# Leaving out waits that other waits contain: a layer kernel (linear attention, then a 4-bit feed-forward) on one core

## What is computed

```python
q, k, v = (split_heads(x @ W + b) for W, b in ((Wq, bq), (Wk, bk), (Wv, bv)))
q, k = (exp(z - max(z)) / (sum(exp(z - max(z))) + EPS) for z in (q, k))
context = ((q @ k.T) / (sum(q) + EPS)) @ v
x = layernorm(x + context @ Wo + bo)
h = silu(fp4_linear(x, w_gate)) * fp4_linear(x, w_up)
x = layernorm(x + fp4_linear(h, w_down))      # fp4_linear rounds both operands
```

## Time and profile before

| | |
|---|---|
| median of 3 runs | 809.0 us (808.98 to 809.23) |
| the profiled execution | 809.8 us |
| its span, first to last instruction | 808.0 us |
| busy: PE, DVE, ACT, POOL | 734.5, 728.9, 577.6, 573.4 us |
| attention loop, passes | 17.1 to 17.7 us each |
| feed-forward loop, passes | 30.0 us each |
| granted TensorE clock, mean | 0.979 |

### The profile page before, as it was taken

One profiled execution on the slowest core, in us unless ns is written; L12 is line 12 of the kernel. 1 busy time (PEld: TensorE's weight loads), 2 busy tenths in 40 slices (PEclk: granted clock), 3 DMA queues, 4 the chain that ended last, 5 costly groups with the idle time before them and its releaser, 6 DMA issues.

```text
span 808.0 us, 19912 instructions
## 1 busy us (share of the span) xinstructions
PE 734.5 (91%) x4964; PEld 689.5 (85%) x4964; DVE 728.9 (90%) x1778; ACT 577.6 (71%) x1547; POOL 573.4 (71%) x617
## 2 busy tenths in 40 slices
PE   4999999999999968799999999999999999999994
PEld 4898888888888847699899899899889889889983
DVE  4989999999999988799999999999999999998883
ACT  3577777778777767477667767677777767767666
POOL 3776666666666655678778878878778788788761
PEclk9999999999999969799999999999999999999998
DMA  4122222222222100000000000000000000000002
GB/s 131 60 72 80 60 71 65 65 65 69 74 70 64 43 27 1 1 1 2 7 21 20 15 19 19 13 19 19 16 17 19 19 13 19 19 13 21 21 21 73
DMA packets 39717, 29.20 MB, mean 36 GB/s; under 512 B 3446, under 2 KB 39676, under 8 KB 39676
## 3 DMA queue, kind: packets, MB, share of 16 engines
q1 hardware_dynamic: 37228, 26.50, 10.6%
q10 hardware_dynamic: 2448, 2.23, 0.9%
HBM read 20.32 MB, written 8.39 MB: 36 GB/s over the span
## 4 chain that ended last, share of the span: by engine, by line
PE 53%; DVE 24%; issue 15%; ACT 2%; POOL 2%; DVEq 2%; DMA 0%; POOLq 0%; ACTq 0%; SPq 0%
PE bank L849 36%; PE wide L849 5%; PE bank L911 3%; DVE ln_u L629 3%; PE bank L857 3%; DVE scratch L837 3%; DVE ln_t L627 3%; DVE scratch L824 2%; PE wide L898 2%; DVE scratch L808 2%; PE wide L952 2%; PE bank L909 2%; DVE scratch L779 1%; DVE rounded L830 1%; DVE res L767 1%
## 5 line engine op out<-in xcount | busy, mean ns | idle before, releaser
L849 PE MATMUL bank<-wf_hi,rounded 128*128 128x352 f32 (+1 forms) x1792 | 411.3, 312 | 34.2 <-DVE rounded L830 21.7
L849 PEld LDWEIGHTS bank<-wf_hi,rounded 128*128 128x128 f32 x1792 | 302.9, 191 | 46.6 <-DVE rounded L830 29.1
L849 PE MATMUL bank<-wf_lo,rounded 128*128 128x352 f32 (+1 forms) x896 | 275.2, 307 | 0.0
L849 PEld LDWEIGHTS bank<-wf_lo,rounded 128*128 128x128 f32 x896 | 171.4, 191 | 0.0
L409 POOL TENSOR_TENSOR scratch<-scratch 128x704 f32<-128x704 f32 x64 | 95.8, 1497 | 97.8 <-DVE scratch L804 97.8
L849 PE MATMUL bank<-qkv_hi,rounded 128*128 128x512 f32 (+1 forms) x512 | 146.6, 341 | 0.0
L351 POOL TENSOR_TENSOR scratch<-scratch 128x512 f32<-128x512 f32 x64 | 67.9, 1060 | 58.8 <-DVE scratch L705 58.7
L849 PEld LDWEIGHTS bank<-qkv_hi,rounded 128*128 128x128 f32 x512 | 94.0, 193 | 10.0
L393 POOL TENSOR_TENSOR scratch<-scratch 128x704 bf16<-128x704 f32 x64 | 100.5, 1570 | 2.6 <-ACT scratch L582 2.6
L416 POOL TENSOR_TENSOR scratch<-scratch 128x704 f32<-128x704 bf16 x64 | 88.8, 1388 | 5.8 <-DVE scratch L808 0.7
L849 PE MATMUL bank<-qkv_lo,rounded 128*128 128x512 f32 (+1 forms) x256 | 87.4, 341 | 0.0
(11 more groups left out here) (102 smaller groups left out, 1745.5 us busy)
## 6 DMA issues: line engine op xcount, KB each, us to landing
scratch<-x_feat SPq DMA_DIRECT2D x64, 128.0 KB, 2.3
scratch<-x_tok SPq DMA_DIRECT2D x64, 128.0 KB, 2.0
out<-scratch SPq DMA_DIRECT2D x64, 128.0 KB, 1.7
scratch<-w_ffn ACTq DMA_DIRECT2D x17, 128.0 KB, 2.1
scratch<-L_attn_Wq SPq DMA_DIRECT2D x1, 256.0 KB, 2.7
scratch<-L_attn_Wk SPq DMA_DIRECT2D x1, 256.0 KB, 2.9
scratch<-L_attn_Wv SPq DMA_DIRECT2D x1, 256.0 KB, 3.8
wo<-L_attn_Wo SPq DMA_DIRECT2D x1, 256.0 KB, 2.9
```

The lines of the kernel that those rows point to most:

```text
L849: last = pe.matmul(dst, x(c), w(c), start=first and n == 0, stop=n == len(terms) - 1)
```

## The change

At 80 places a wait is taken out that another wait of the same or an earlier instruction already contains, by way of a chain of semaphores. No instruction that computes or moves data is changed, added or moved, and the order on each engine stays. The core of the diff, with the places that the steps of the prediction speak of:

```diff
@@ gpsimd, attention @@
                         need(pool, a_rec, m - 1)
-                        need(pool, a_post, m - 3)
                         pool.tensor_tensor(heads(feat[b]), prob[b][:, :, 0:HD], over(hrec[b], 2 * NH, HD),
                                            ALU.mult).then_inc(a_feat, 1)
...
                         need(pool, a_xhi, m + 3)
-                        need(pool, a_qkv, m + 2 - T + 1)
                         pool.tensor_tensor(xt_lo[s], xt_raw[s], xt_hi[s].bitcast(F32),
@@ gpsimd, ffn @@
                         need(pool, h_q, m - 2)
-                        need(pool, h_c, m - 2)
-                        need(pool, h_y, m - 2)
                         need(pool, h_inv, m)
                         pool.tensor_tensor(blocks(hxn[b1]), blocks(hid[b1]), over(binv[b1], NB),
...
-                        need(pool, h_sc, m - 1)
-                        need(pool, h_t, m - 3)
                         need(pool, h_g, m - 1)
@@ scalar @@
             def row_sums(n, norm, ready, sm):
                 at = bass.ds(n + norm * NT, 1)
-                need(act, sm, n)
-                if norm == 1 and isinstance(n, int) and n == 0:
-                    act.wait_ge(a_sm, NT)
                 need(act, ready, n + 1)
...
-                        need(act, a_post, m - 2)
                         need(act, a_out, m - 3 - T + 1)
                         act.activation(qt_hi[s], pqt[b1][:, 0:KC * P].rearrange("p (c n) -> p c n", c=KC),
...
-                        need(act, w_cs, i)
-                        need(act, w_gs, i)
                         need(act, w_ys, i + 1)
                         act.activation(w_mg, w_y, ACT.Copy, bias=FLOOR, scale=STEP).then_inc(w_mgs, 1)
                     if t == 1 and live_seq(i, 0, NW) and live_seq(i, 1, NW):
-                        need(act, w_max, i + 1)
-                        need(act, w_xns, i + 1)
                         act.dma_start(w_raw, w_ffn.rearrange("j p n -> (j p) n")[bass.ds((i + 1) * P, P), :]
@@ vector @@
                         need(dve, a_qhi, m - 2)
-                        need(dve, a_out, m - 3 - T + 1)
                         dve.tensor_tensor(qt_lo[s], pqt[b1][:, 0:KC * P].rearrange("p (c n) -> p c n", c=KC),
@@ tensor, ffn @@
                         need(pe, x_lo, m + 1)
-                        need(pe, h_a, m)
                         gate_up(0, b).then_inc(gu_a, 1)
```

More of the change, by code:

```diff
@@ L537, in ffn @@
                         need(act, gu_b, m)
-                        need(act, h_b, m - 1)
                         act.activation(gated[1], pg[1][:, 0:HALF], ACT.Silu).then_inc(si_b, 1)
@@ L542, in ffn @@
                         need(act, e_xns, p + 1)
-                        need(act, e_mgs, p - 1)
                         act.activation(e_y[e], e_xn[e], ACT.Square, scale=BOWL).then_inc(e_ys, 1)
@@ L551, in ffn @@
                         need(act, gu_a, m + 1)
-                        need(act, h_a, m)
                         act.activation(gated[0], pg[0][:, 0:HALF], ACT.Silu).then_inc(si_a, 1)
@@ L555, in ffn @@
                         need(act, h_t, m - 2)
-                        need(act, d_s, m - 4)
                         act.activation(hqt_hi[b1][:, :, :], wide[:, 0:IP].rearrange("p (c n) -> p c n", c=IC),
@@ L560, in ffn @@
                         need(act, x_t, m + 2)
-                        need(act, gu_b, m)
                         act.activation(xqt_hi[b1][:, :, :], pxt[:, 0:KC * P].rearrange("p (c n) -> p c n", c=KC),
@@ L573, in ffn @@
                         need(act, h_xn, m)
-                        need(act, h_mg, m - 2)
                         act.activation(hy[b1], hxn[b1], ACT.Square, scale=BOWL).then_inc(h_y, 1)
@@ L670, in attention @@
                         need(dve, w_cs, i + 1)
-                        need(dve, w_qs, i)
                         dve.tensor_tensor(w_g, w_c, w_mg, ALU.subtract).then_inc(w_gs, 1)
@@ L687, in attention @@
                         need(dve, a_exp, m)
-                        need(dve, a_rec, m - 2)
                         dve.tensor_reduce(hsum[b1], prob[b1], axis=AX_X, op=ALU.add).then_inc(a_sum, 1)
@@ L703, in attention @@
                         need(dve, a_sum, m)
-                        need(dve, a_feat, m - 2)
                         dve.reciprocal(hrec[b1], hsum[b1]).then_inc(a_rec, 1)
@@ L707, in attention @@
                         need(dve, a_post, T * i)
-                        need(dve, a_c, i - 1)
                         dve.tensor_tensor(kv_m, pkv[:, 0:KC * P].rearrange("p (c n) -> p c n", c=KC),
@@ L713, in attention @@
                         need(dve, w_s2s, i + 2)
-                        need(dve, w_xns, i + 1)
                         dve.reciprocal(w_inv, w_s2).then_inc(w_invs, 1)
@@ L723, in attention @@
                         need(dve, a_chi, i)
-                        need(dve, a_out, T * (i - 1))
                         dve.tensor_tensor(c_lo[:, :, :], pc.rearrange("p (c n) -> p c n", c=KC),
@@ L753, in ffn @@
                         p, e = pair(i, t, 6)
-                        if isinstance(i, int):
-                            dve.wait_ge(a_x1, 2 * p + 2 if i < B_LOOP[0] - 1 else NT)
                         need(dve, e_scs, p - 1)
-                        need(dve, e_s2s, p - 1)
                         dve.tensor_reduce(e_mx[e], blocks(res[:, bass.ds(p * 2 * D, 2 * D)]), axis=AX_X,
@@ L761, in ffn @@
                         need(dve, si_b, m)
-                        need(dve, h_xn, m - 2)
                         dve.tensor_tensor(hid[b1][:, HALF:I], gated[1], pu[1][:, 0:HALF], ALU.mult).then_inc(h_b, 1)
@@ L771, in ffn @@
                         need(dve, e_max, p + 1)
-                        need(dve, e_invs, p - 1)
                         dve.tensor_scalar(e_s2[e], e_mx[e], SHY / 6.0, TINY * SHY, ALU.mult,
@@ L784, in ffn @@
                         need(dve, e_mgs, p + 1)
-                        need(dve, e_gs, p - 1)
                         dve.tensor_tensor(e_c[e], e_xn[e], e_mg[e], ALU.add).then_inc(e_cs, 1)
@@ L788, in ffn @@
                         need(dve, h_max, 2 * m)
-                        need(dve, h_inv, m - 2)
                         dve.tensor_scalar(bs2[b1], bmx[b1], SHY / 6.0, TINY * SHY, ALU.mult, ALU.max).then_inc(h_s2, 1)
@@ L793, in ffn @@
                         need(dve, e_s2s, p + 1)
-                        need(dve, e_xns, p - 1)
                         dve.reciprocal(e_inv[e], e_s2[e]).then_inc(e_invs, 1)
@@ L806, in ffn @@
                         need(dve, h_c, m - 1)
-                        need(dve, h_q, m - 3)
                         dve.tensor_tensor(hg[b], hc[b], hmg[b], ALU.subtract).then_inc(h_g, 1)
@@ L816, in ffn @@
                         need(dve, h_hi, m - 2)
-                        need(dve, d_s, m - 4)
                         dve.tensor_tensor(hqt_lo[b1][:, :, :], wide[:, 0:IP].rearrange("p (c n) -> p c n", c=IC),
@@ L828, in ffn @@
                         need(dve, x_hi, m + 2)
-                        need(dve, gu_b, m)
                         dve.tensor_tensor(xqt_lo[b1][:, :, :], pxt[:, 0:KC * P].rearrange("p (c n) -> p c n", c=KC),
@@ L835, in ffn @@
                         need(dve, e_cs, p + 1)
-                        need(dve, x_q, 2 * (p - 1))
                         dve.tensor_tensor(e_g[e], e_c[e], e_mg[e], ALU.subtract).then_inc(e_gs, 1)
@@ L882, in attention @@
                         need(pe, w_qs, i)
-                        need(pe, a_clo, min(i - 2, NS) if isinstance(i, int) else i - 2)
                         for c in range(KC):
@@ L895, in attention @@
                         need(pe, a_kvm, i)
-                        need(pe, w_los, min(i, NW) if isinstance(i, int) else i)
                         for c in range(KC):
@@ L956, in ffn @@
                         need(pe, x_q, m + 2)
-                        need(pe, x_lo, m + 1)
                         for c in range(KC):
```

40 lines of the change are left out of this document (removed).

## The result

The change makes the kernel 0.28% faster: the ratio of after to before is 0.9972, with a 95% interval of 0.9965 to 0.9979 (medians 807.9 and 810.2 us, 20 runs each). That is 2.3 us (1.7 to 2.8). The forecast was 4.6. The direction was right, and about half of the gain came. The 804.4 was taken off a median of 809.0 from 3 runs; 20 runs of the same kernel have 810.2, and off that the forecast would be 805.6. The measured 807.9 lies inside the stated range of 800.2 to 808.2, at its upper end, where the prediction had put the rival "all become long".

A forecast was written before the change was run, and what follows sets the result against it. DVE was taken to pace the attention loop, with a race against POOL on their shared interface. Gains of 1.7+1.8+0.5+0.4+0.2 = 4.6 us off the 809.0 median gave 804.4, range 800.2 to 808.2.

The forecast's parts named there:

- all become long: Rival, attention loop: POOL gains 0.02 and all passes become long; 2.8-1.8 = 1.0 us gain, 808.0; chance 0.08.
- TensorE has a reserve in each pass: 0.29 us: Attention loop: TensorE idles 0.29 us per pass waiting for DVE's c_lo, just enough for all passes to become short.
- The price of a wait: Any engine: a separate wait released last costs 0.06 us; one satisfied earlier costs nothing while the engine still works.
- The rule of the wait queue: Skill's rule behind the nothing-changes rival: queued waits are all overlapped, so time stays 809.0; chance 0.08.
- The four relays: Attention pass: L443 starts 0.14 behind L655, L649 0.02 behind L472, L486 0.02 behind L482, L351 0.08 behind L705.
- ACT runs without a gap from there to L472: Attention pass: L443's 0.06 us gain carries through ACT to L472, whose end releases DVE L649.
- POOL's lead changes by 0.01 at most: Attention-loop race: L629 comes 0.14 us earlier, L357 0.13 to 0.15, so POOL's 0.01 to 0.04 lead barely changes.
- three passes turning short: Attention loop: the race leans slightly to DVE, turning three of nine long passes short; 3 x (17.66-17.05) = 1.8 us.
- The 0.14 of a pass: Attention loop: DVE reaches L629 0.06+0.08 us earlier, so each pass shortens by 0.14; 12 x 0.14 = 1.7 us.
- The rest: Outside the attention loop: four other attention passes 0.5 us, feed-forward loop 0.4, drain 0.2.
- the carrier that I named for feed-forward: Feed-forward loop: POOL L409 starts earlier in one tile of four; 0.03 us a pass, 12 x 0.03 = 0.4.
- The rival "slower": Attention loop: POOL L351 gets ahead of DVE L631, making a new stop; 12 x 0.45 = 5.4, 811.6; chance 0.06.

The follow-up runs named there:

- e2: Kernel before with only three removals: a_post before POOL L351, a_sm before ACT L443, a_out before DVE L649; 803.8 us, ratio 0.9921.
- e3: Kernel before with only these removed: w_cs, w_gs before ACT L486; w_max, w_xns before ACT's DMA issue; a_post before ACT L472; 809.7 us, ratio 0.9994.
- e5: Changed kernel with five waits put back, those that hold POOL L357 back; 803.4 us, ratio 0.9917 to the kernel before.
- e12: e5 with one two-operand layer-norm step (DVE L625) moved ahead of the reciprocal L705, in the loop alone; 798.7 us, ratio 0.9848 to the kernel before.
- e9: Changed kernel with the first instruction of ACT's attention loop at position 0 of an instruction memory block; 807.6 us, ratio 0.9971 to the kernel before.
- e8: Changed kernel with one wait put back, a_post before POOL L351; 809.0 us, ratio 0.9978 to the kernel before.
- e1: Kernel before with only the attention removals and the shared row sums and squares; feed-forward keeps its waits; 808.6 us, ratio 0.9981.
- e4: Changed kernel with DVE's layer-norm step L629 moved ahead of q_lo (L649); 808.6 us, ratio 0.9982 to the kernel before.
- e11: e5 with the first instruction of ACT's attention loop at position 0; 802.1 us, ratio 0.9901 to the kernel before.

## Why the prediction fell short, step by step

Two steps failed: the way from L443 to L472, taken to be without a gap, and the lead that was to change by 0.01 at most. The second had the price. The others held, or were off in size.

- **What bounds the kernel: right, with one wrong reserve.** DVE paces the loop, and long and short passes differ by the stop of old L629 behind POOL; e2, e3 and e5 show it by turning the race either way. "TensorE has a reserve in each pass: 0.29 us" was wrong as a limit. It was one idle gap of PE, for which the earlier trace rows name "issue" and not c_lo, and e12 took 1.2 us off a long pass before PE was full. All gaps of PE in a long pass sum to 0.81 us (17.66 less 16.85 busy), and even that is too little, as its busy time shrank as well. The reserve is read from a run in which the pacer is gone.
- **The price of a wait: right.** The four relays came out at 0.15, 0.03, 0.03 and 0.07 us against a forecast of 0.14, 0.02, 0.02 and 0.08. The rule of the wait queue, by which nothing changes, is refuted by e2, which takes out waits alone and is 6.4 us faster.
- **The first step that failed: "ACT runs without a gap from there to L472".** L443 did start 0.05 earlier, but ACT's loop turn lies on that way and became 0.076 longer, so L472 starts 0.02 later than before. e9 gives it back by the place of the loop's head alone. So DVE reached old L629 0.06 earlier, not 0.14.
- **The second, with the price: "POOL's lead changes by 0.01 at most".** POOL gained 0.16 to 0.20 (forecast 0.13 to 0.15), DVE 0.06. The lead went from 0.02 to 0.05 up to 0.14 to 0.17, and the 1.8 us of three passes turning short became a loss: eight long passes gained 0.18 each in the mean, three short ones lost 0.42 each, the last gained 0.21, in all 0.39. The forecast had 1.7 plus 1.8 there. This is the rival "all become long", which had 0.08. e9 adds that it would have come about without the turn as well, with a lead of 0.07: an estimate that two shifts cancel to 0.01 was worth nothing, as the smallest leads needed only that much to turn, and both ways. Nor were there "nine leads of about 0.02 to 0.05": the ninth long pass is the last (17.43 us, lead 0.14), and the first has a lead of 0.12. In e2 and e5 both still stand still.
- **The 0.14 of a pass: near in size, wrong in reason.** A long pass got 0.16 to 0.20 shorter, but by POOL's side: old L357 moved by as much, pass by pass. A stopped L629 ends with POOL's instruction, so the pass follows POOL and ACT, and what DVE gains ahead of it is worth nothing: e8 moved it by 0.08 and the pass by 0.01.
- **The rest: near in size.** Passes outside the twelve: 33.53 to 33.31 us for the two ahead of them and 18.66 to 18.57 for the one behind, 0.3 against 0.5. Feed-forward 0.35 in ten passes (forecast 0.3), drain 97.09 to 96.75 (0.3 against 0.2). DVE L735 (old L804) to POOL L394 (old L409), the carrier that I named for feed-forward, moved only from 0.17 to 0.15 in one tile of four:

```profile
488.14 0.37 DVE L735 RECIPROCAL scratch<-scratch 128x44 f32<-128x44 f32 x1
...
488.66 1.48 POOL L394 TENSOR_TENSOR scratch<-scratch 128x704 f32<-128x704 f32 x1 [0.79 <-DVE scratch L735]
```

  The 0.03 of a pass lies in DVE's own queue, in another tile. Before, and then after (L728, L735, L738 are old L795, L804, L808):

```profile
473.83 0.34 DVE L795 RECIPROCAL scratch<-scratch 128x32 f32<-128x32 f32 x1
...
474.13 0.43 DVE L804 RECIPROCAL scratch<-scratch 128x44 f32<-128x44 f32 x1
474.48 0.46 DVE L808 TENSOR_TENSOR scratch<-scratch 128x704 bf16<-128x704 bf16 x1
```

```profile
472.71 0.34 DVE L728 RECIPROCAL scratch<-scratch 128x32 f32<-128x32 f32 x1
...
472.98 0.42 DVE L735 RECIPROCAL scratch<-scratch 128x44 f32<-128x44 f32 x1
473.32 0.46 DVE L738 TENSOR_TENSOR scratch<-scratch 128x704 bf16<-128x704 bf16 x1
```

  L804 starts 0.30 behind L795 before and 0.27 after, L808 0.65 and 0.61. In the mean of the ten passes, counted from L615, all that DVE does ahead of this L804 stands where it stood, and all behind L808 comes 0.03 to 0.04 earlier. In e1, which keeps these waits, it stays within 0.01. So here waits that had been satisfied cost 0.03 though DVE was at work, which the prediction had at nothing.
- **What stays open.** The profiled executions differ by 1.8 us. 0.7 of it lie ahead of the first DVE old L709 (32.65 us before, 31.99 after), and that start scatters: 31.23 in e5 and 32.57 in e12, whose programs are the same up to there. The stages behind it sum to 1.1, and in this sum the changeover stands as a loss of 0.3 us (116.5 to 116.8), for which the prediction had nothing; over the runs it takes 115.1 to 117.0. The interval of the medians is 1.7 to 2.8. Whether the removals shorten the start or lengthen the changeover isn't settled.
- **The rival "slower", a new stop behind POOL L351,** didn't happen in the loop. The same mechanism, the stop handed to the next step, is what undid e4.

## What to carry to other kernels

Where two engines share an interface, what a step costs is read from who starts first there: list the leads over all passes, the first and the last too, say which edit moves which racer, and treat a lead as open when it is smaller than the shifts that the edits can bring (here up to 0.2 us). Removing waits on the racer that should lose can be harmful, even if each removal is sound: five of the 80 cost this change 4.4 us. Keep them, or better, move the small two-operand step to where the other engine runs nothing, and look at which step comes next. What an engine gains ahead of such a stop is lost in it.

## What the runs showed of the hardware that I had not expected

- The race on the shared interface is decided within some 0.02 us. In the kernel before, POOL's L357 leading by 0.019 left L629 at 0.148, leading by 0.025 held it for 0.727, until POOL's end. No run has a case between. Where POOL led by less than 0.02 and still lost, it took 0.74 to 0.77 instead of 0.73; with DVE 0.02 or more in front it took its 0.73. The Trainium skill (SBUF — State Buffer, "SBUF: two separate sides") calls it an exclusive lock that the first one holds for its whole instruction; the long passes agree, with 0.59 to 0.73 us before and after for a step of 0.15.
- ACT's loop turn is 0.161 us or 0.237 to 0.259 us for the same body, by the place of its first instruction; in every changed program but e9 and e11, whose loop head was laid at 0, it was 0.236 or more (e2 takes out three waits and has 0.245). The Trainium skill (Runtime: NRT & Kernel Launch, "Instruction fetch mechanics") says that a taken branch whose target isn't held in the instruction memory waits for its fetch; no run here shows what was fetched.
- An instruction that holds the wait itself started 0.03 us behind its releaser on ACT (L457) and DVE (L603); with the same wait in an instruction of its own ahead of it, it was 0.11 (old L486) and 0.12 (old L649). On POOL old L351 it was 0.07 against 0.16.
